# GpSimd pauses between bursts of gathers with a fill of its own, where it waited for the last gather to land

## The chip, the cores and the metric

The kernel runs on one core of a Trainium2 chip. A time is the device time of one execution in microseconds (us), and the program is compared by medians of several executions. One execution of the kernel was also recorded by the hardware profiler. Engines go by the names of the profile: PE is TensorE (PEld its weight loads), DVE is VectorE, ACT is ScalarE, POOL is GpSimd, SP is SyncE.

## The reference

A recommendation tower over a batch of 2048. Every sample has 40 ids, one for each of 40 embedding tables of 1,000 to 125,000 rows by 32 columns. All 780 pairs of fields are joined by a bilinear form, and the 780 results and 16 dense inputs go through a small network:

```
x  = stack([tbl_f[ids[:, f]] for f in range(40)])          # 2048 x 40 x 32
out = einsum('bpd,pde,bpe->bp', x[:, i], bilinear, x[:, j])  # 780 pairs i < j
y  = relu(relu([out, dense_ctx] @ W_top1 + b1) @ W_top2 + b2) @ W_top3
```

## The kernel before

The batch is cut into five **blocks** of 256, 512, 512, 512 and 256 rows (`ROWS`), numbered 0 to 4. The 40 fields are ten **chunks** of four fields, so that four times 32 columns fill 128 partitions. A **unit** is a pair of chunks, 50 in all; PE multiplies one chunk's transposed embeddings with the bilinear matrices (line 841, and 850 for a chunk with itself, into `U`), DVE multiplies the result with the other chunk's embeddings (line 740, `prod`), and PE sums that over partitions (line 866, `bank_z`). One such step over 512 columns is a **cycle**: 25 cycles in block 0, 50 in blocks 1 to 3, 25 in block 4, 200 in all. `summed` counts finished cycles. The network's layers (line 892) for a block are laid between the cycles of the next.

Embeddings come in two ways. Fourteen small tables lie in SBUF and are read by a product with a one-hot matrix, which DVE makes (line 704, `ones`) from the ids spread over the partitions (`idx_wide`, loads on SP's queue of up to 500 KB) and PE multiplies (line 792, `misc`). In block 0 seven of the fields come so, later all fourteen. All other fields are **gathered**: POOL issues an indirect DMA of 128 rows by 32 columns (line 505) for each field and each 128 samples, into the tile `rows`, which has seven slots (`R_SLOTS`). A slot holds one **turn**: the gathered fields of one chunk of one block. When all of a turn has landed (`gathered`), PE transposes it (line 815), and ACT copies the transpose to `x_T` (line 550), which the cycles read. There are 45 turns and 430 gathers. Turns 0 to 7 have eight gathers each and turn 8 has two (block 0). Blocks 1 to 3 have nine turns each of 16, 8, 8, 8, 16, 16, 12, 16 and 4 gathers, and block 4 half of that. So turn 1 is complete with gather 16, turn 2 with 24, turn 3 with 32, turn 4 with 40, turn 13 with 122, turn 14 with 138, turn 16 with 166 and turn 23 with 242.

What sets the order: each engine runs its instructions in program order. PE's order is written out (`TURN_AT` gives the cycle after which a turn is transposed), and a turn that has not landed stops everything that stands behind it on PE. POOL's order is that of the turns. It waits for three things: that PE has emptied a slot (`turned`), that PE has come to a cycle from which a field may be fetched (`summed`, the table `DUE`, from block 0's last turns on, some 0.8 of a block ahead of its use), and, behind every fourth gather but in turn 0 (`BURST = 4`), that this gather has landed. The first such wait stands behind gather 12; there are 105 of them.

SP issues all plain loads in one order: four small tables and the bilinear matrices `W`, most of them in rows of 128 bytes, then `idx_wide`, more tables, more of `W`, and from 69 us on the first layer's weights.

Of the kernel before, what the change touches and what calls it, by code (L numbers as in the profile page):

```python
# [12 lines left out]
P = 128  # L13
# [11 lines left out]
NB = max(ROWS)  # L25
# [243 lines left out]
X_SLOTS, R_SLOTS, P_SLOTS, Z_SLOTS, ONES = 12, 7, 6, 10, 4  # L269
# [12 lines left out]
def dlrm_tower(nc, dense_ctx, ids, tables, W_top1, b_top1, W_top2, b_top2, W_top3, bil, out):  # L282
    with ExitStack() as ctx:
        def sb(name, shape, dt=F32):
            return ctx.enter_context(nc.sbuf_tensor(name, shape, dt))

        def ps(name, shape):
            return ctx.enter_context(nc.psum_tensor(name, shape, F32))

        def sem(name):  # L290
            return ctx.enter_context(nc.semaphore(name))
# [22 lines left out]
        h1 = sb("h1", [P, H1 // P, NB])  # L314
        h2 = sb("h2", [P, H2 // P, NB])
        y = sb("y", [1, NB])

        prods = prod[:].rearrange("p s r n -> p (s r n)")
        spare_z = z[:, ZT:, :].rearrange("p s n -> p (s n)")
# [14 lines left out]
        bank_z = ps("bank_z", [P, NB])  # L334
        misc = ps("misc", [P, NB])

        ids_loaded, ids_rest_loaded = sem("ids_loaded"), sem("ids_rest_loaded")
        W_zeroed, stage_zeroed, W1_zeroed = sem("W_zeroed"), sem("stage_zeroed"), sem("W1_zeroed")
        late_stage_zeroed = sem("late_stage_zeroed")
# [11 lines left out]
        gathered = [sem(f"gathered{s}") for s in range(R_SLOTS)]  # L351
# [131 lines left out]
        @block.gpsimd  # L483
        def _(pool):
            nc.gpsimd.memset(ident[:], 0.0).then_inc(ident_made, 1)
            nc.gpsimd.iota(row_of_i[:], pattern=[[1, KC]], base=0, channel_multiplier=KC).then_inc(row_of_made, 1)
            pool.wait_ge(ident_made, 1)
            nc.gpsimd.affine_select(out=ident[:], in_=ident[:], compare_op=ALU.not_equal, fill=1.0, base=0,
                                    pattern=[[-1, P]], channel_multiplier=1).then_inc(ident_made, 1)
            pool.wait_ge(ids_loaded, 16)  # L490
            begun = [0] * R_SLOTS
            for n, (o, c) in enumerate(TURNS):
                if n == 1:
                    pool.wait_ge(misc_kept, JOB[("look", 0, 0)] + 1)
                if n >= R_SLOTS:
                    pool.wait_ge(turned, n - R_SLOTS + 1)
                for f in GATHERED[(o, c)]:
                    field = CF * CHUNK_OF_STEP[c] + f
                    if DUE[(o, c, f)]:
                        pool.wait_ge(summed, DUE[(o, c, f)])  # L500
                    if n == FIRST_TURN[1] and f == GATHERED[(o, c)][0]:
                        pool.wait_ge(ids_rest_loaded, 16)
                        pool.wait_ge(rows_zeroed, 1)
                    for t in range(ROWS[o] // P):
                        nc.gpsimd.indirect_dma_start(  # L505
                            out=rows[:, n % R_SLOTS, t, f, :], out_offset=None, in_=tables[field][:, :],
                            in_offset=bass.IndirectOffsetOnAxis(
                                ap=idx[:, OFF[o] // P + t, field:field + 1], axis=0),
                        ).then_inc(gathered[n % R_SLOTS], 16)
                        begun[n % R_SLOTS] += 1  # L510
                        if sum(begun) % BURST == 0 and n > 0:
                            pool.wait_ge(gathered[n % R_SLOTS], 16 * begun[n % R_SLOTS])

        @block.scalar
        def _(act):
# [26 lines left out]
            def keep_turn(o, c):  # L542
                n, N = TURN[(o, c)], ROWS[o]
                at = 2 * (U_USE[("turn", o, c)] % U_SLOTS)
                J = CHUNK_OF_STEP[c]
                if free_of(o, J):
                    act.wait_ge(multiplied, free_of(o, J))
                act.wait_ge(turned, n + 1)
                for _, lo, hi in pieces([CF * J + f for f in GATHERED[(o, c)]]):
                    last = nc.scalar.activation(x_of(o, J)[lo * DIM:hi * DIM, :], U[lo * DIM:hi * DIM, at, 0:N],  # L550
                                                ACT.Copy)
                last.then_inc(turn_kept, 1)
# [415 lines left out]
```

## Time and profile before

| | us |
|---|---|
| median of 3 runs | 867.06 (866.54 to 875.61) |
| profiled execution, its own time | 871.17 |
| its span, first to last instruction | 869.4 |
| PE matmuls busy | 779.0 |
| DVE busy | 586.5 |
| POOL busy (the gathers' issue) | 416.9 |
| ACT busy | 199.1 |
| mean granted TensorE clock | 0.941 |

The span is one execution; the 1.8 us between it and the execution's own time lie outside the first and last instruction. A gather's bar on POOL is the time in which its transfer is made up and issued; its data land later. The granted clock is 1.0 or 0.5 at any moment (2.4 or 1.2 GHz), and a figure between is a mean.

### The profile page before, as it was taken

Reading aid. Unit: us, or ns where it says so; the run is one execution under the profiler, and the core shown is the slowest. Engines: PE = TensorE matmul, PEld = TensorE weight load, DVE = VectorE, ACT = ScalarE, POOL = GpSimd, SP = SyncE. Lnnn points to the kernel's source line nnn. Section 1 sums busy time; section 2 is a strip of 40 time slices with the busy share of each in tenths; the row PEclk is TensorE's granted clock in tenths of the full one; section 3 lists DMA queues with packets and bytes.
Section 4 is the critical chain, followed back from the end, with each engine's and each line's share of the span. In section 5 each row is a group of like instructions: output and inputs, shape, how many; then the busy total and the mean of one; then the engine's idle time right before and its main releaser. Section 6 shows DMA issues by size and latency. Waiting matters only on the chain.

```text
span 869.4 us, 16025 instructions
## 1 busy us (share of the span) xinstructions
PE 779.0 (90%) x6766; PEld 308.5 (35%) x6766; DVE 586.5 (67%) x702; ACT 199.1 (23%) x362; POOL 416.9 (48%) x437
## 2 busy tenths in 40 slices
PE   3357888999679899989999999999999999999999
PEld 3124444443223233323323323323323234445446
DVE  5245766668448879857758679757768589566660
ACT  6022212232112023043021032132210221322212
POOL 5445456555656555555655565656565652310000
PEclk9567899799789999999999999999999999999999
DMA  4582330020010101020100101020100100000000
GB/s 90 115 114 52 68 69 11 11 29 17 14 25 11 33 12 27 12 35 11 28 11 12 34 11 28 12 24 12 19 12 12 23 11 16 8 5 2 2 1 1
DMA packets 62562, 22.53 MB, mean 26 GB/s; under 512 B 45283, under 2 KB 61677, under 8 KB 62490
## 3 DMA queue, kind: packets, MB, share of 16 engines
q1 hardware_dynamic: 48702, 14.37, 7.7%
q0 software_dynamic: 13760, 7.07, 6.9%
q8 instruction: 53, 0.87, 0.4%
q14 instruction: 19, 0.16, 0.1%
q10 hardware_dynamic: 28, 0.06, 0.0%
HBM read 21.40 MB, written 0.07 MB: 25 GB/s over the span
## 4 chain that ended last, share of the span: by engine, by line
PE 58%; POOL 15%; issue 11%; DMA 10%; DVE 3%; another core or an unknown queue 2%; ACT 1%; POOLq 0%; DVEq 0%; ACTq 0%
PE U L841 17%; PE bank_z L866 16%; POOL rows L505 15%; PE misc L892 14%; DMA rows<-in_tbl,idx 10%; PE misc L792 6%; DVE prod L740 2%; PE U L850 2%; PE U L892 2%; PE U L815 1%; DVE ones L704 1%; ACT x_T L559 0%; PE bank_z L874 0%; DMA idx<-in_ids 0%
## 5 line engine op out<-in xcount | busy, mean ns | idle before, releaser
L505 POOL DMA_INDIRECT rows<-in_tbl,idx x430 | 416.1, 968 | 351.0 <-DMA rows<-in_tbl,idx 203.0
L740 DVE TENSOR_TENSOR prod<-U,x_T 128x1024 f32<-128x1024 f32 (+1 forms) x314 | 342.6, 1127 | 102.4 <-PE U L841 84.5
L866 PE MATMUL bank_z<-prod,select 128*32 128x512 f32 (+1 forms) x2000 | 226.5, 540 | 4.0 <-ACT z L539 2.3
L841 PE MATMUL U<-x_T,W 32*128 32x512 f32 (+1 forms) x1440 | 203.6, 568 | 16.1 <-ACT x_T L550 9.3
L704 DVE TENSOR_SCALAR ones<-idx_wide,row_of 125x2048 bf16<-125x2048 f16 (+3 forms) x180 | 108.2, 627 | 63.4 <-PE misc L792 43.3
L792 PE MATMUL misc<-ones,tabs 125*32 125x512 bf16 (+1 forms) x1890 | 125.2, 356 | 7.0 <-issue 5.8
L740 DVE TENSOR_TENSOR prod<-U,x_look 128x1024 f32<-128x1024 f32 (+1 forms) x90 | 88.0, 1003 | 44.1 <-PE U L841 39.2
L841 PEld LDWEIGHTS U<-x_T,W 32*128 32x128 f32 x1440 | 79.0, 193 | 102.1 <-issue 52.1
L892 PE MATMUL misc<-z,W 128*128 128x512 f32 (+1 forms) x238 | 106.3, 561 | 0.6 <-ACT x_look L559 0.6
L866 PEld LDWEIGHTS bank_z<-prod,select 128*32 128x32 f32 x2000 | 46.8, 112 | 154.1 <-issue 110.8
L792 PEld LDWEIGHTS misc<-ones,tabs 125*32 125x32 bf16 x1890 | 65.2, 100 | 85.8 <-issue 55.8
L550 ACT ACTIVATE x_T<-U 32x512 f32<-32x512 f32 (+5 forms) x52 | 26.7, 514 | 235.5 <-PE U L815 149.9
L815 PE MATMUL U<-ident,rows 128*128 128x128 f32 x144 | 27.3, 306 | 44.9 <-DMA rows<-in_tbl,idx 43.2
L892 PEld LDWEIGHTS misc<-z,W 128*128 128x128 f32 x238 | 39.4, 189 | 66.8 <-issue 61.3
L539 ACT ACTIVATE z<-bank_z 128x512 f32<-128x512 f32 (+1 forms) x35 | 17.9, 512 | 180.2 <-PE bank_z L866 137.7
L841 PE MATMUL U<-x_look,W 32*128 32x512 f32 (+1 forms) x360 | 55.0, 551 | 0.3 <-DVE prod L740 0.3
L577 ACT ACTIVATE x_twin<-x_T 32x512 f32<-32x512 f32 (+1 forms) x80 | 43.4, 542 | 2.5 <-DVE prod L728 1.4
L815 PEld LDWEIGHTS U<-ident,rows 128*128 128x128 f32 x144 | 17.8, 153 | 67.1 <-issue 59.3
L892 PE MATMUL misc<-h,W 128*128 128x512 f32 (+3 forms) x80 | 37.6, 586 | 0.0
L722 DVE TENSOR_TENSOR prod<-U,x_T 128x512 f32<-128x512 f32 (+1 forms) x20 | 11.6, 579 | 38.3 <-PE U L850 28.7
L850 PE MATMUL U<-x_twin,W 32*64 32x512 f32 (+1 forms) x200 | 36.4, 607 | 0.1
L850 PE MATMUL U<-x_T,W 32*64 32x512 f32 (+1 forms) x160 | 28.9, 609 | 1.4 <-ACT x_twin L587 1.4
(70 smaller groups left out, 270.6 us busy)
## 6 DMA issues: line engine op xcount, KB each, us to landing
rows<-in_tbl,idx POOLq DMA_INDIRECT x430
idx_wide<-idx_rows SPq DMA_DIRECT2D x6, 500.0 KB
idx_wide<-idx_rows SPq DMA_DIRECT2D x6, 375.0 KB
idx_wide<-idx_rows SPq DMA_DIRECT2D x3, 187.5 KB
W<-in_W_top SPq DMA_DIRECT2D x35, 2.0 KB
W<-_L_rec_bilinear_matrices SPq DMA_DIRECT2D x4, 128.0 KB
W<-in_W_top SPq DMA_DIRECT2D x1, 512.0 KB
idx_wide<-idx_rows SPq DMA_DIRECT2D x2, 250.0 KB
```

The lines of the kernel that those rows point to most:

```text
L505: nc.gpsimd.indirect_dma_start(out=rows[:, n % R_SLOTS, t, f, :], out_offset=None, in_=tables[field][:, :], in_offset=bass.IndirectOffsetO ...
L539: nc.scalar.activation(z[:, at % Z_SLOTS, 0:ROWS[o]], bank_z[:, 0:ROWS[o]], ACT.Copy).then_inc(z_kept, 1)
L550: last = nc.scalar.activation(x_of(o, J)[lo * DIM:hi * DIM, :], U[lo * DIM:hi * DIM, at, 0:N], ACT.Copy)
L577: nc.scalar.activation(x_twin[r * DIM:(r + 1) * DIM, 1, 0:N], x_of(o, a + 1)[(CF - 1 - r) * DIM:(CF - r) * DIM, :], ACT.Copy)
L704: nc.vector.tensor_scalar(ones[:, n % ONES, 0:len(fs), 0:N], idx_wide[job % 2][:, 0:len(fs), 0:N], row_of[0:KP, k:k + 1], None, ALU.is_equ ...
L740: last = nc.vector.tensor_tensor(to[:, :, m * N:(m + n) * N].rearrange("p r (m n) -> p r m n", m=n), U[:, at:at + 2, m * N:(m + n) * N].re ...
L792: last = nc.tensor.matmul(misc[f * DIM:(f + 1) * DIM, 0:N], tabs[0:KP, LOOKED.index(field), part, k * DIM:(k + 1) * DIM], ones[:, n % ONES ...
L815: last = nc.tensor.transpose(U[:, at, t * P:(t + 1) * P], rows[:, n % R_SLOTS, t].rearrange("p f d -> p (f d)"), ident[:])
L841: last = nc.tensor.matmul(U[:, at + r % 2, m * N:(m + 1) * N], W[row, at_W:at_W + P], x_of(o, a)[row, :], start=True, stop=True, skip_grou ...
L850: last = nc.tensor.matmul(U[side * P // 2:(side + 1) * P // 2, at + r % 2, m * N:(m + 1) * N], W[row, at_W + side * P // 2:at_W + (side + ...
L866: last = nc.tensor.matmul(bank_z[r * DIM:(r + 1) * DIM, 0:N], sel, prod[:, (2 * g + r // 2) % P_SLOTS, r % 2, m * N:(m + 1) * N], start=(k ...
L892: last = nc.tensor.matmul(res, lhs, rhs, start=(t == 0), stop=(t == depth - 1), skip_group_check=True)
```

## The change

The wait for landing goes. In its place POOL fills a new tile `pause` of 128 x 512 float32 with zeros and waits until this fill is done, which a semaphore of its own (`paused`) tells. Nobody reads `pause`. The place is the same: behind every fourth gather but in turn 0, 105 times. The waits on `turned`, `summed` and the ids stay, and PE still waits for all gathers of a turn.

```diff
+        pause = sb("pause", [P, NB])
...
+        paused = sem("paused")
...
-            begun = [0] * R_SLOTS
+            begun, pauses = [0] * R_SLOTS, 0
...
                         if sum(begun) % BURST == 0 and n > 0:
-                            pool.wait_ge(gathered[n % R_SLOTS], 16 * begun[n % R_SLOTS])
+                            pauses += 1
+                            nc.gpsimd.memset(pause[:], 0.0).then_inc(paused, 1)
+                            pool.wait_ge(paused, pauses)
```

## Rows read from the trace of the kernel before

**Rows 1.** the page: the span, and who carries the chain that ended last

```profile
span 869.4 us, 16025 instructions
...
PE 58%; POOL 15%; issue 11%; DMA 10%; DVE 3%; another core or an unknown queue 2%; ACT 1%; POOLq 0%; DVEq 0%; ACTq 0%
```

**Rows 2.** PE's waits over the span: us in total, times, longest

```profile
PE U L815 <- DMA rows<-in_tbl,idx: 43.2, 7, 12.8
```

**Rows 3.** PE's timeline: turns' transposes: start us, us, what [idle before <-releaser]

```profile
38.10 0.66 PE L815 MATMUL U<-ident,rows 128*128 128x128 f32 x2 [12.82 <-DMA rows<-in_tbl,idx]
...
54.32 0.66 PE L815 MATMUL U<-ident,rows 128*128 128x128 f32 x2 [10.07 <-DMA rows<-in_tbl,idx]
...
68.59 0.41 PE L815 MATMUL U<-ident,rows 128*128 128x128 f32 x2
...
84.11 0.66 PE L815 MATMUL U<-ident,rows 128*128 128x128 f32 x2 [0.44 <-DMA rows<-in_tbl,idx]
...
226.99 0.87 PE L815 MATMUL U<-ident,rows 128*128 128x128 f32 x3 [8.49 <-DMA rows<-in_tbl,idx]
...
253.97 0.87 PE L815 MATMUL U<-ident,rows 128*128 128x128 f32 x3 [6.11 <-DMA rows<-in_tbl,idx]
...
305.02 0.63 PE L815 MATMUL U<-ident,rows 128*128 128x128 f32 x4 [3.24 <-DMA rows<-in_tbl,idx]
...
435.63 0.87 PE L815 MATMUL U<-ident,rows 128*128 128x128 f32 x3 [2.04 <-DMA rows<-in_tbl,idx]
```

**Rows 4.** GpSimd's timeline while the loads run: gathers 12, 13, 22 and 24

```profile
22.57 0.94 POOL L505 DMA_INDIRECT rows<-in_tbl,idx  x1 [0.30 <-issue]
28.65 0.94 POOL L505 DMA_INDIRECT rows<-in_tbl,idx  x1 [5.13 <-DMA rows<-in_tbl,idx]
...
47.13 1.40 POOL L505 DMA_INDIRECT rows<-in_tbl,idx  x1 [0.31 <-issue]
...
50.16 0.94 POOL L505 DMA_INDIRECT rows<-in_tbl,idx  x1 [0.30 <-issue]
```

**Rows 5.** GpSimd's timeline in a quiet stretch: one burst ends, the next starts

```profile
220.58 0.94 POOL L505 DMA_INDIRECT rows<-in_tbl,idx  x1 [0.30 <-issue]
223.21 0.94 POOL L505 DMA_INDIRECT rows<-in_tbl,idx  x1 [1.68 <-DMA rows<-in_tbl,idx]
224.46 0.95 POOL L505 DMA_INDIRECT rows<-in_tbl,idx  x1 [0.31 <-issue]
```

**Rows 6.** GpSimd's waits over the span, columns as in Rows 2

```profile
POOL rows L505 <- DMA rows<-in_tbl,idx: 203.0, 93, 5.3
...
POOL rows L505 <- PE bank_z L866: 37.8, 17, 5.0
```

**Rows 7.** GpSimd's timeline, first and eighth gather of turn 0

```profile
3.06 1.10 POOL L505 DMA_INDIRECT rows<-in_tbl,idx  x1 [1.65 <-DMA idx<-in_ids]
...
12.71 1.49 POOL L505 DMA_INDIRECT rows<-in_tbl,idx  x1 [0.30 <-issue]
```

**Rows 8.** GpSimd's timeline, two of its fills at the start

```profile
0.25 0.10 POOL L957 MEMSET const-float32-0.0<- 128x1 f32 x1 [0.25 <-issue]
...
0.74 0.20 POOL L485 MEMSET ident<- 128x128 f32 x1 [0.29 <-POOLq L957]
```

**Rows 9.** stretches: length, busy us by engine, granted clock, DMA share, GB/s

```profile
60.00:166.00 106.00, 88.05 (x956) 44.35 (x948) 69.80 (x103) 20.31 (x45) 57.01 (x59) 0.84 0.26 49
227.00:230.80 3.80, 3.80 (x16) 1.39 (x20) 0.60 (x1) 0.60 (x1) 1.84 (x2) 0.50 0.05 9
254.00:258.10 4.10, 4.10 (x28) 1.18 (x28) 1.00 (x2) 0.60 (x1) 1.16 (x2) 0.50 0.06 12
305.00:309.30 4.30, 4.28 (x29) 0.96 (x29) 1.85 (x3) 0.60 (x1) 1.73 (x2) 0.60 0.07 11
435.50:439.00 3.50, 3.37 (x24) 1.25 (x28) 0.23 (x1) 0.60 (x1) 0.94 (x1) 0.51 0.08 14
```

**Rows 10.** the page, costliest groups: VectorE's one-hot compares

```profile
L704 DVE TENSOR_SCALAR ones<-idx_wide,row_of 125x2048 bf16<-125x2048 f16 (+3 forms) x180 | 108.2, 627 | 63.4 <-PE misc L792 43.3
```

## The prediction, made before the result was known

> **What bounds the kernel now.** I read the page first. The chain that ended last is PE for 58% of the span, but POOL and the gathers' transfers hold 25% of it between them [rows 1]. A chain led by two sides asks for the places where they meet, so next come PE's waits: 43.2 us go to gathers that had not landed, in seven waits [rows 2]. PE's timeline shows where. Turn 1 costs 12.82 us, turn 2 10.07, turn 4 0.44, and later turns 13, 14, 16 and 23 cost 8.49, 6.11, 3.24 and 2.04 [rows 3]. Turn 3 costs nothing. From 436 us on no turn is waited for. So up to turn 16 POOL sets the pace at two places, the beginning and the middle of block 1, and PE sets it elsewhere and from there to the end.
>
> Why is POOL late? A gather occupies it for 0.94 us and the next begins 0.30 later; behind every fourth stands the gap in which it waits for landing. In a quiet stretch that gap is 1.68 us [rows 5]; while SP's loads run it is 5.13 [rows 4]. Over the span the waits that a landing ended make 203.0 us, 93 of them, 2.18 each, while waits for PE's progress make only 37.8 [rows 6]. A burst thus takes 4 x 0.94 + 3 x 0.30 + g = 4.66 + g, with g the gap. The change touches g alone.
>
> **The new gap.** It has three pieces: from gather to fill, the fill, from fill to gather. No row has a fill of 128 x 512. One of 128 x 1 took 0.10 us and one of 128 x 128 took 0.20 [rows 8]; the straight line through them gives 0.10 + 0.10 x 511/127 = 0.50, four times the larger 0.82. For the two joints I take at most the 0.30 that stands between gathers. So g lies between 0.50 (no joints) and 1.42 (0.82 + 0.60), and I take 0.50 + 0.60 = 1.1, because the line through both fills uses all that the trace has. The gain per burst is 0.6 us when quiet and up to 4 while loads run. The Trainium skill, page "SBUF — State Buffer", section "SBUF: two separate sides", gives GpSimd 4 bytes per lane and cycle at 1.2 GHz, so an estimate from that page is 512 / 1.2 GHz = 0.43 us for the fill; the sum would move by under half a microsecond.
>
> **First part, turns 1 to 4.** Gather 12 ends at 22.57 + 0.94 = 23.5 [rows 4]. Gather 16 then ends at 23.5 + 1.1 + 4.66 = 29.3 and gather 24 two bursts of 5.76 later, at 40.8. When do they land? Behind gather 12 it took 5.1 us from the end of its bar, behind gather 24 3.2 (bar's end 51.1, turn 2 at 54.32) [rows 3, 4]; in the quiet stretch 1.7 [rows 5]. I take 4.0, the middle of the two busy ones, and keep 1.7 and 5.1 as ends. Turn 2 then starts at 44.8 in place of 54.3. From turn 2 to turn 3 PE needed 68.59 - 54.32 = 14.3 us and waited for no gather; from 3 to 4 it needed 84.11 - 0.44 - 68.59 = 15.1 [rows 3]. That is PE's own work with its looks and cycles, and it becomes the bound here: turn 3 at 59.1 (gather 32 would have landed by 40.8 + 11.5 + 4 = 56.3), turn 4 at 74.2 (gather 40 by 67.8). **Gain 9.9 us.** Its ends: g 0.5 and landing 1.7 give 13.5, g 1.4 and 5.1 give 7.5. Of turn 1's wait of 12.82 and turn 2's of 10.07 more than half stays, since gathers at 1.25 us apiece are slower than the few cycles that PE has to do by then.
>
> **Second part, the later turns.** Gather 122, the last of turn 13, now ends 24.5 bursts behind gather 24, at 40.8 + 24.5 x 5.76 = 181.9. PE comes to turn 13 at 227.0 - 8.5 - 9.9 = 208.6, so it waits no longer, with 27 us to spare. Gather 166 (turn 16) ends at 245, PE comes at about 274; gather 242 (turn 23) at 355, PE at about 401. So all four waits go: 8.49 + 6.11 + 3.24 + 2.04 = **19.9 us**. What becomes late next is POOL's own gate: with gathers ahead, it waits for `summed`, as it did for 37.8 us before [rows 6]. That costs nothing, since this gate opens a good half of a block before the turn. The gain saturates here: any g up to about 2.0 removes these waits, because the 27 us are spread over 27.5 bursts. That makes the sum insensitive to the fill's length.
>
> **Third part, the clock.** Behind each of these four waits PE worked at the lower of its two clocks for a while: 227.0 to 230.8 at 0.50, 254.0 to 258.1 at 0.50, 305.0 to 309.3 at 0.60, 435.5 to 439.0 at 0.51 [rows 9]. It was busy all that time. Time at half clock is 3.8 + 4.1 + 4.3 x 0.8 + 3.4 = 14.7 us, and without the idle time ahead of it the same work takes half: **7.4 us**. Lower end 0. For turns 1 and 2 I take none back, since PE still idles ahead of them.
>
> **The sum.** 9.9 + 19.9 + 7.4 = 37.2 us. The profiled execution took 871.2, so a like one takes 834.0; it lay 4.1 above the median of 867.06, so the median becomes 829.9. I say 830. What lies outside the span is not touched. The fills themselves, 105 x 0.5 us, lie on POOL and in the place of a longer wait. `pause` has no reader and adds no work elsewhere.
>
> **Rivals.**
> *The start gives nothing.* Without the wait the gathers queue behind SP's loads, and landing, not issue, sets the pace of turns 1 and 2. For it: landing took up to 5.1 us there. Against it: turn 0's eight gathers went out with no wait, the eighth 9.65 us behind the first, 1.38 apiece against 1.24 [rows 7]. Only 19.9 + 7.4 remain: 840. Chance 0.12.
>
> *The clock gives more.* From 60 to 166 us the granted clock is 0.84 on average with PE busy 88.05 of 106 us [rows 9]; that is 34 us at half clock. If PE, less often halted, kept the full clock, up to half of that, 17 us, comes on top: 813. Against it: no gather is waited for between 85 and 218 us, so PE's idle bits there have other causes and stay. Chance 0.08.
>
> *Fills and one-hots hold each other up.* A gather at 47.13 took 1.40 us where 0.94 is usual [rows 4]; one-hot compares run close by. They are busy 108.2 of 869.4 us, 12% [rows 10]. The same page of the Trainium skill, section "Who interferes with whom", has VectorE's compares and copies in a two-port mode and GpSimd shut each other out for a whole instruction. As a mechanism of this kernel: 12% of 105 fills is 13 meetings, each worth at most a compare of some 0.63 us on average, 8 us in all if every one lay on the path: 838. DVE idles a third of the span, so most would be hidden. The 0.46 us by which that gather is longer agree with such a rule, and do not prove it. Chance 0.06.
>
> *The gap hardly shrinks.* If going from gather to fill and back costs POOL more than joints of 0.30, g can be near 2.4, the old mean, and nothing comes: 858 to 867. Chance 0.06.
>
> *Slower: the fill takes longer than the landing did.* Place: every burst up to turn 23. Before, turn 16 started at 305.0 [rows 3], so its gather 166 ended some 1.7 earlier, at 303.3; 38.5 bursts lie between gather 12 and it, so the old pace equals 4.66 + g with g = (303.3 - 23.5) / 38.5 - 4.66 = 2.6. This is the point from which it decides. At g = 3.0 turn 16 comes at 23.5 + 38.5 x 7.66 + 1.7 = 320, 15 later; the 19 bursts to turn 23 take 145.5 us against 130.6 before, 15 more; block 3, with slack before, adds about 10 (an estimate): 40 in all, 907. For it: no row shows a fill between gathers. Against it: the fill would have to take over 2 us, four times my line. Chance 0.08.
>
> **How the numbers follow.** My forecast, 822 to 838, has 0.60. The cases with the start's gain gone or the locks hold 0.18 and reach 840, with their own spread some 848; the clock's case reaches 813, less the spread 811. So 811 to 848 leaves out 0.06 + 0.08 and a little of the tails. About 1% is what a measurement of this kernel can tell from none: faster 0.85, within 1% 0.07, slower 0.08.
>
> **What the profile after would show.** Fills of about 0.5 us, and 1.1 us from the end of one burst to the next. Turn 1 near 33, turn 2 near 45, turn 4 near 74 us. No wait of PE for gathers after turn 2. On POOL, waits on `summed` (bank_z) that grow well beyond 37.8 us. A granted clock of 1.0 at what was 227, 254, 305 and 436 us. I am wrong if a fill with its joints takes over 2 us, if a gather's bar grows beyond 0.94 as more are in flight, or if PE, come earlier, meets something else that is late: `W` of a chunk or `idx_wide`, whose loads are not moved by the change.

## The result: slower on the measured chip, 890.86 us against 867.29

The changed kernel took 890.86 us (median of 4 runs, 887.7 to 895.35), the kernel before 867.29 us (4 runs, 866.54 to 875.61). The ratio is 1.0265, 95% interval 1.0193 to 1.0337: slower beyond the noise, though the interval does not settle whether by more than 2%. The forecast was 830 us, with a range of 811 to 848. The profiled execution took 891.69 us, its span is 889.9.

GpSimd did what the change asks of it. Its timeline in the changed kernel, the end of one burst and the start of the next:

```profile
33.52 0.94 POOL L507 DMA_INDIRECT rows<-in_tbl,idx  x1 [0.30 <-issue]
34.45 0.54 POOL L515 MEMSET pause<- 128x512 f32 x1
35.27 0.95 POOL L507 DMA_INDIRECT rows<-in_tbl,idx  x1 [0.27 <-issue]
...
39.96 0.54 POOL L515 MEMSET pause<- 128x512 f32 x1
```

The fill takes 0.54 us here (0.58 on average over all 105), it starts at once behind the gather, and 0.27 us lie between it and the next gather. The gap behind a burst is 0.81 us. A burst with its gap takes 39.96 - 34.45 = 5.51 us, or 1.38 us per gather. The old gap was 1.68 when quiet [rows 5].

PE's waits in the changed kernel (us in total, times, longest) and then GpSimd's:

```profile
PE U L845 <- ACT x_T L554: 20.5, 5, 13.9
PE U L845 <- issue: 14.3, 8, 5.8
PE U L819 <- DMA rows<-in_tbl,idx: 12.2, 2, 6.5
```
```profile
POOL rows L507 <- PE bank_z L870: 172.1, 70, 6.5
```

The waits for gathers fell from 43.2 to 12.2 us [rows 2], and only turns 1 and 2 are waited for. GpSimd now runs ahead until its own gate stops it, 172.1 us against 37.8 [rows 6]. Two new lines stand above: PE waits for ACT's copy of a transposed turn, and for "issue", which means that the profile shows no end of a wait. The chain that ended last says the same, and names a new holder:

```profile
PE 71%; another core or an unknown queue 14%; DVE 5%; ACT 4%; issue 4%; DMA 1%; DVEq 0%; ACTq 0%
```

POOL and the gathers' transfers held 25% of the old chain [rows 1] and are next to nothing in this one, whose 1% of DMA is put down to loads of `idx_wide`. "Another core or an unknown queue" held 2% and holds 14%, though the program runs on one core. The timelines show where that is. PE's, from turn 2 to the first cycles behind turn 3:

```profile
44.04 0.66 PE L819 MATMUL U<-ident,rows 128*128 128x128 f32 x2 [6.52 <-DMA rows<-in_tbl,idx]
50.50 2.11 PE L845 MATMUL U<-x_T,W 32*128 32x256 f32 x16 [5.80 <-issue]
...
73.07 1.01 PE L796 MATMUL misc<-ones,tabs 125*32 125x512 bf16 x5 [0.40 <-issue]
74.50 1.01 PE L796 MATMUL misc<-ones,tabs 125*32 125x512 bf16 x5 [0.42 <-issue]
75.93 0.64 PE L796 MATMUL misc<-ones,tabs 125*32 125x512 bf16 x4 [0.43 <-issue]
...
82.23 0.69 PE L819 MATMUL U<-ident,rows 128*128 128x128 f32 x2
96.78 2.11 PE L845 MATMUL U<-x_T,W 32*128 32x256 f32 x16 [13.86 <-ACT x_T L554]
```

ACT's, its copies of turns 2 and 3:

```profile
50.07 0.39 ACT L554 ACTIVATE x_T<-U 128x256 f32<-128x256 f32 x1 [16.96 <-remote]
...
96.34 0.38 ACT L554 ACTIVATE x_T<-U 128x256 f32<-128x256 f32 x1 [41.78 <-remote]
```

And GpSimd's over the same stretch, around its last gather ahead of the gate:

```profile
93.58 0.96 POOL L507 DMA_INDIRECT rows<-in_tbl,idx  x1 [0.30 <-issue]
101.01 0.94 POOL L507 DMA_INDIRECT rows<-in_tbl,idx  x1 [6.47 <-PE bank_z L870]
```

PE's transposes of turn 2 end at 44.70, and ACT, which has nothing else to do, copies them at 50.07. Those of turn 3 end at 82.92 and are copied at 96.34, that is 13.4 us later. GpSimd has issued gathers in bursts without a longer break since turn 0; its last one ends at 94.54, and ACT goes on 1.8 us behind it. The releaser is shown as "remote": the profile sees the semaphore change without an instruction that ends just then. In between PE also works thinly: four or five matmuls come every 1.43 us and then it stands, marked "issue". That mark must be read with care: the 5.80 us of it ahead of 50.50 ended 0.04 us behind ACT's copy (50.07 + 0.39), which this matmul needs, so it was a wait for ACT whose end the trace does not hold. VectorE waits for PE in the same way, `ones` "remote" 47.1 us in 12 waits, the longest 15.0. I call this the **hold** below.

So turn 3 came at 82.23 instead of the forecast 59.1, and PE was granted only half its clock from 60 to 100 us (0.50 in the windows 60 to 80 and 80 to 100, in which it was busy for 12.8 and 5.1 us of 20).

### The profile page after: what moved, and what is told of

Read it like the earlier page. It is cut to its first block, busy times and chain, and to the rows that moved or that the text cites. A ratio compares the mean times of both kernels' runs of the same rounds, so it can differ in the third digit from the quotient of the medians.

```text
span 889.9 us, 16130 instructions
## 1 busy us (share of the span) xinstructions
PE 791.1 (89%) x6766; PEld 311.7 (35%) x6766; DVE 592.2 (67%) x702; ACT 199.2 (22%) x362; POOL 481.1 (54%) x542
## 4 chain that ended last, share of the span: by engine, by line
PE 71%; another core or an unknown queue 14%; DVE 5%; ACT 4%; issue 4%; DMA 1%; DVEq 0%; ACTq 0%
PE U L845 22%; PE bank_z L870 20%; PE misc L896 15%; PE misc L796 8%; PE U L854 3%; DVE prod L744 3%; PE U L819 2%; PE U L896 1%; DVE ones L708 1%; ACT x_twin L581 1%; DMA idx_wide<-idx_rows 1%; ACT x_T L563 1%; ACT x_twin L584 0%; ACT x_T L554 0%
## 5 line engine op out<-in xcount | busy, mean ns | idle before, releaser
L507 POOL DMA_INDIRECT rows<-in_tbl,idx x430 | 419.9, 976 | 307.3 <-PE bank_z L870 172.1
L708 DVE TENSOR_SCALAR ones<-idx_wide,row_of 125x2048 bf16<-125x2048 f16 (+3 forms) x180 | 113.4, 657 | 83.6 <-remote 47.1
L796 PE MATMUL misc<-ones,tabs 125*32 125x512 bf16 (+1 forms) x1890 | 132.6, 364 | 7.1 <-issue 5.0
L896 PE MATMUL misc<-z,W 128*128 128x512 f32 (+1 forms) x238 | 108.5, 571 | 6.5 <-ACT x_look L563 6.3
L896 PEld LDWEIGHTS misc<-z,W 128*128 128x128 f32 x238 | 40.4, 193 | 74.2 <-issue 63.6
L515 POOL MEMSET pause<- 128x512 f32 x105 | 60.7, 578 | 0.1
L845 PE MATMUL U<-x_look,W 32*128 32x512 f32 (+1 forms) x360 | 58.0, 554 | 1.0 <-DVE prod L744 0.9
L543 ACT ACTIVATE z<-bank_z 128x512 f32<-128x512 f32 (+1 forms) x35 | 17.9, 512 | 175.4 <-PE bank_z L870 132.1
L819 PE MATMUL U<-ident,rows 128*128 128x128 f32 x144 | 26.1, 297 | 14.0 <-DMA rows<-in_tbl,idx 12.2
L854 PE MATMUL U<-x_T,W 32*64 32x512 f32 (+1 forms) x160 | 30.8, 573 | 1.6 <-issue 1.6
L845 PEld LDWEIGHTS U<-x_look,W 32*128 32x128 f32 x360 | 22.7, 188 | 24.5 <-issue 13.4
```

What stands on the lines that cost most here:

```text
L507: nc.gpsimd.indirect_dma_start(out=rows[:, n % R_SLOTS, t, f, :], out_offset=None, in_=tables[field][:, :], in_offset=bass.IndirectOffsetO ...
L515: nc.gpsimd.memset(pause[:], 0.0).then_inc(paused, 1)
L708: nc.vector.tensor_scalar(ones[:, n % ONES, 0:len(fs), 0:N], idx_wide[job % 2][:, 0:len(fs), 0:N], row_of[0:KP, k:k + 1], None, ALU.is_equ ...
L796: last = nc.tensor.matmul(misc[f * DIM:(f + 1) * DIM, 0:N], tabs[0:KP, LOOKED.index(field), part, k * DIM:(k + 1) * DIM], ones[:, n % ONES ...
L819: last = nc.tensor.transpose(U[:, at, t * P:(t + 1) * P], rows[:, n % R_SLOTS, t].rearrange("p f d -> p (f d)"), ident[:])
L845: last = nc.tensor.matmul(U[:, at + r % 2, m * N:(m + 1) * N], W[row, at_W:at_W + P], x_of(o, a)[row, :], start=True, stop=True, skip_grou ...
```

## The experiments

The same kernels behave differently from chip to chip, so each result names its chip by number (0, 4, 5, 7 or 12). Each ratio is to the kernel before, run in turns with it on the same chip. The chip of the first measurement is not on record. Chip 5 served two jobs and behaved alike in both; the others served one job each, so for them chip and moment are not told apart.

### First job, chip 5: the pace of the gathers

My theory was that PE's results are held up while gathers follow each other too closely.

**no_pause**: neither the wait nor a fill.

```diff
-                        if sum(begun) % BURST == 0 and n > 0:
-                            pool.wait_ge(gathered[n % R_SLOTS], 16 * begun[n % R_SLOTS])
```

> Neither the wait for landing nor the fill; gathers follow each other at 1.25 us apiece (the changed kernel: 1.37 on average, 5.5 for four with the fill). Pace theory: PE is held up whenever gathers follow each other closely for more than a few in a row, and in the changed kernel PE's bundles of matmuls came every 1.43 us in that state; at 1.25 us apiece it is held longer, so slower than the changed kernel's 891, I expect 895 to 920. Fill theory (the fill itself does the harm, by a lock or by its place on POOL): without fills the loss goes, 825 to 845.

Measured 782.06 us, ratio 0.913 (0.9096 to 0.9165). That lies outside both ranges. The fastest pace of all gave the best time: my theory, as it stood, fell.

**fill_each_256**: half the fill, behind every gather, 0.36 us each.

```diff
-                        if sum(begun) % BURST == 0 and n > 0:
+                        if n > 0:
                             pauses += 1
-                            nc.gpsimd.memset(pause[:], 0.0).then_inc(paused, 1)
+                            nc.gpsimd.memset(pause[:, 0:NB // 2], 0.0).then_inc(paused, 1)
```

> A fill of 128x256 behind every gather from turn 1 on, in place of one of 128x512 behind every fourth: 0.94 + 0.32 + 0.27, about 1.53 us from gather to gather, evenly spread, no wait for landing. Pace theory: 1.53 is above the 1.43 us at which PE's bundles came, so PE is hardly held up, and POOL is still faster than before (1.7 on average): 825 to 845. Landing theory (what matters is that a gather has landed, and the queue is empty, before more are issued while SP's loads run): as slow as the changed kernel, 880 to 900. Fill theory: four times as many fills, slower than 891.

Measured 822.41 us, 0.9604 (0.9564 to 0.9644), a little below the range of the theory of pace.

**four_fills**: four whole fills behind each burst.

```diff
+                            for _ in range(4):
-                            pauses += 1
-                            nc.gpsimd.memset(pause[:], 0.0).then_inc(paused, 1)
-                            pool.wait_ge(paused, pauses)
+                                pauses += 1
+                                nc.gpsimd.memset(pause[:], 0.0).then_inc(paused, 1)
+                                pool.wait_ge(paused, pauses)
```

> Four fills of 128x512 behind every fourth gather, 2.2 us in a row, about 7.1 us for four gathers (before: 6.4 when quiet, up to 9.8 while SP's loads run); no wait for landing. Pace theory: PE is held up as little as before; POOL's pace is near the old mean, so 855 to 875. Landing theory: slow at the start, 880 to 900. Fill theory: 420 fills in place of 105, over 900.

Measured 905.93 us, 1.0567 (1.0515 to 1.0619). PE waits 105.7 us for gathers in 17 waits. The range of the theory on the fill fits, but these waits are what grew: this is the plain price of slow gathers.

**wait_block0**: the landing wait in turns 1 to 8, fills from turn 9.

```diff
-                        if sum(begun) % BURST == 0 and n > 0:
+                        if sum(begun) % BURST == 0 and 0 < n < FIRST_TURN[1]:
+                            pool.wait_ge(gathered[n % R_SLOTS], 16 * begun[n % R_SLOTS])
+                        elif sum(begun) % BURST == 0 and n > 0:
                             pauses += 1
```

> The wait for landing stays for turns 1 to 8 (block 0, while SP's loads run), fills take its place from turn 9 on. Load theory (the harm is done by gathers in flight beside SP's loads): the start is as before, the later waits of PE for gathers go, 840 to 855. Pace theory: the start is as before, and from turn 9 on PE is held up as in the changed kernel, where it lost in block 1 what it gained at gathers: 860 to 880.

Measured 821.97 us, 0.959 (0.9544 to 0.9635), faster than both ranges. On this chip the kernels stand in the order of their gathers' pace, and the kernel before took 856 us, not 867. Either the recorded result was not of this kind of chip, or the changed kernel is odd. So it was run itself.

### Second job, chip 5: the changed kernel itself

> The changed kernel itself, once more. In the recorded run of it PE's semaphore updates came up to 14 us behind the end of its matmuls, and in the four experiments so far none came over 0.11 us late. Chip theory (those late updates belong to the chip or the moment on which the two kernels were first compared, and gathers without a pause for landing only make them worse): with no late updates here the working of the prediction holds, 812 to 830, ratio about 0.96. Kernel theory (one fill of 128x512 behind every fourth gather brings them about, which no experiment had from the start on): late updates again, ratio 1.02 to 1.03.

Measured 792.05 us, ratio **0.9244** (0.9222 to 0.9267). There are no late updates, as the chip theory has it, and it is 20 us below that theory's range.

> The kernel before, once more, for its trace beside after_again's. Chip theory: no update of PE over 0.2 us late (in the first trace up to 4 us, all through the span), and with that about 856, the median of before in the last job. Kernel theory: updates up to 4 us late as in the first trace.

Measured 857.0 us, 0.9997 (0.997 to 1.0023).

> No pause of either kind, once more, to see whether its 782 stands on this chip beside the changed kernel. Chip theory: if updates of PE are late here, it is hit harder than any other, since its gathers have no gap at all, and could be over 890; if they are not, 782 again. Pace theory on a chip without late updates: the faster the gathers, the better, no_pause 782, the changed kernel between it and before.

Measured 781.86 us, 0.9131 (0.9107 to 0.9155).

The same code that lost 2.7% gains 7.6% here. PE's timeline in the changed kernel on chip 5, from turn 2 to turn 3, and ACT's copies of these turns:

```profile
44.59 0.66 PE L819 MATMUL U<-ident,rows 128*128 128x128 f32 x2 [7.04 <-DMA rows<-in_tbl,idx]
45.72 2.11 PE L845 MATMUL U<-x_T,W 32*128 32x256 f32 x16 [0.47 <-ACT x_T L554]
...
54.93 2.13 PE L796 MATMUL misc<-ones,tabs 125*32 125x512 bf16 x36
56.98 0.44 PE L819 MATMUL U<-ident,rows 128*128 128x128 f32 x2
57.97 1.13 PE L845 MATMUL U<-x_T,W 32*128 32x256 f32 x8 [0.55 <-ACT x_T L554]
```
```profile
45.29 0.38 ACT L554 ACTIVATE x_T<-U 128x256 f32<-128x256 f32 x1 [11.75 <-PE U L819]
...
57.46 0.38 ACT L554 ACTIVATE x_T<-U 128x256 f32<-128x256 f32 x1 [7.68 <-PE U L819]
```

Turn 2 is transposed within 0.6 us of the other chip's, and copied when its transposes end. The releaser has a name, PE U L819. 36 matmuls of the looks come in one row of 2.13 us. Turn 3 stands at 56.98. No engine has a single wait that ends "remote" in any of the ten profiles taken on chips 5 and 7, and no copy of a turn by ACT starts over 0.10 us behind its transposes.

### Third job, chip 7: the two halves, and the fill's length

**fill_block0** is wait_block0 the other way round: fills in turns 1 to 8, the landing wait from turn 9.

> Fills for turns 1 to 8 (block 0), waits for landing from turn 9 on: the complement of wait_block0. Where no update of PE is late: wait_block0 kept the start of the kernel before and reached 822, the whole change 792; so the start is worth 30 and the rest 35, and this one should be 857 - 30 = 827, within 6, if the two parts add. If the waits of PE for gathers in block 1 only shift (a PE that is earlier meets the same late gathers), less: 840 to 850. If updates of PE are late again, both this and the changed kernel are above before.

Measured 826.38 us, 0.9644 (0.9597 to 0.9692). With wait_block0 the parts add up: 30.1 us from the start and 34.4 from the later turns (856.32 - 821.97, chip 5) make the 64 us of the whole.

**short_fill** has the whole change, with a fill of 128x1.

```diff
-                            nc.gpsimd.memset(pause[:], 0.0).then_inc(paused, 1)
+                            nc.gpsimd.memset(pause[:, 0:1], 0.0).then_inc(paused, 1)
```

> The changed kernel with a fill of 128x1 in place of 128x512: the gap behind a burst falls from about 0.81 us to about 0.4. The working of the prediction says that POOL's pace past turn 2 no longer matters, so only turns 1 and 2 come sooner, by 1 to 2 us: 790, and 782 (no pause) is the floor. Port theory (the fill's length holds VectorE up): most of the 10 us between the changed kernel and no pause comes back, 782 to 785.

Measured 781.82 us, 0.9132 (0.91 to 0.9164), the time of no_pause.

> The changed kernel once more, on whichever chip this job gets. If it is the same one as in the last two jobs: 792 again. If it is another: chip theory says that 792 (ratio 0.924) or 891 (ratio 1.03) comes with the absence or presence of late updates of PE in its trace, and with nothing in between.

Measured 792.99 us, 0.9256 (0.922 to 0.9292). So the length of the fill costs 11 us, about what I had put for a fill that holds VectorE up. Some of it is gathers that come later: PE waits 18.3 us for them against 12.5. Some is VectorE, whose largest compare is longer; with no fill at all (no_pause) it takes 770 ns. How the 11 us split between the two is not shown. Groups by shape, of short_fill and then of after_third:

```profile
L708 DVE TENSOR_SCALAR ones<-idx_wide,row_of 125x2048 bf16<-125x2048 f16 x60 | 44.2, 759 | 20.8 <-PE misc L796 15.1 <-DMA idx_wide<-idx_rows 5.7
```
```profile
L708 DVE TENSOR_SCALAR ones<-idx_wide,row_of 125x2048 bf16<-125x2048 f16 x60 | 46.9, 804 | 20.6 <-PE misc L796 15.1 <-DMA idx_wide<-idx_rows 5.4
```

### Fourth job, chip 4: the hold again

> The changed kernel once more, to meet the late updates of PE again. Two chips have given 792 and 793 with none over 0.2 us. Chip theory: if this job lands where updates are late, 885 to 895 and ratio 1.02 to 1.04; if not, 792 again.

Measured 898.77 us, **1.0294** (1.0236 to 1.0352). The kernel before took 874.56.

> No pause, beside it. Where updates of PE are late: if gathers that follow each other without a gap are what holds them, it is above the changed kernel, over 895; if it is the fills that hold them, it is below before. Where they are not late: 782 again, which tells nothing new.

Measured 902.79 us, 1.0348 (1.0286 to 1.041): the kernel that gained 8.7% on chips 5 and 7. Its PE timeline shows the hold at its purest; three of fifteen rows of one matmul each:

```profile
41.93 0.59 PE L790 MATMUL misc<-ones,tabs 125*32 125x512 bf16 x1 [2.54 <-issue]
44.73 0.59 PE L790 MATMUL misc<-ones,tabs 125*32 125x512 bf16 x1 [2.21 <-issue]
...
78.33 0.37 PE L813 MATMUL U<-ident,rows 128*128 128x128 f32 x1 [2.43 <-issue]
```

One matmul every 2.80 us, for 39 us. GpSimd's last gather ahead of its gate ends at 78.75. VectorE restarts at 86.78 and ACT at 87.07, both "remote", after 55.74 and 53.65 us without work. What grows is the gap ahead of the matmul. Its bar of 0.59 us, at a granted clock of 0.50, has an end that the profile models, so it can't show a slower matmul. The Trainium skill, page "SBUF — State Buffer", section "SBUF: two separate sides", says that a DMA cannot slow a compute instruction or the other way round. VectorE's bars agree: its products of 128x1024 from `x_T` took 1216 ns on average in the changed kernel both with the hold (first measurement) and without (chip 5). The page says nothing of the gap, which is what costs here.

### Fifth job, chip 12: what in the stream of gathers makes the hold

Open was whether the break's length, the pace, or SP's weight loads beside the first turns decides. The control told which kind of chip it was.

> The changed kernel, to tell which kind of chip this is. If TensorE's updates arrive late here: 1.027 to 1.030 of the kernel before, turn 3 transposed at 80 to 100 us. If they don't: 0.925, turn 3 at 57 us, and then the other three kernels of this job only repeat what they gave.

Measured 890.87 us, 1.0205 (1.0151 to 1.0259), a chip with the hold. The ratio is a little better than I had put it and turn 3 came at 70.70, ahead of the 80 to 100. Here the long wait stands behind it: ACT copied it at 95.1, 23.2 us behind its transposes.

> Four fills of 0.54 us behind each burst instead of one, so that GpSimd's break of some 2.9 us is longer than that of the landing wait, with no wait for a transfer in it. On a chip with late updates: if the length of the break is what lets TensorE's updates through, the first turns keep the time of the kernel before (turn 3 transposed at 65 to 75 us, no ScalarE copy over 4 us behind its transposes) and the ratio is the 1.057 of the other kind of chip or a little below, 1.04 to 1.06. If the landing wait itself is needed, turn 3 comes at over 80 us and the ratio is 1.06 to 1.10. On a chip without late updates: 1.057.

Measured 911.13 us, 1.0451 (1.0396 to 1.0506), turn 3 at 66.21. There is no landing wait in it, and the start keeps the old pace; the loss is PE's 87.9 us of waits for gathers. No copy by ACT came over 2.7 us late. Breaks made of fills do what the landing wait did.

> A fill of 128x256 (0.36 us) behind every gather: no bursts, breaks of some 0.6 us, the same average pace as with the landing wait. On a chip with late updates: if the break's length decides, none is long enough, turn 3 comes at over 75 us and the ratio is 1.00 to 1.05; if the pace decides, turn 3 comes at 60 to 65 us and the ratio is 0.96 to 0.98. On a chip without late updates: 0.960.

Measured 825.17 us, **0.9468** (0.9418 to 0.9518). "The break's length decides" fell: breaks of 0.6 us were enough, turn 3 stood at 64.66 us, and the ratio is a little better than the range that went with the pace. PE's waits for gathers are 34.5 us, and the chain is PE 73% with "another core or an unknown queue" at 0%.

> The landing wait in turns 1 to 8, fills from turn 9 on. On a chip with late updates: if the loss lies in the first eight turns (between turns 2 and 9 the changed kernel lost 47 us on the kernel before, and from turn 9 to the end it gained some 15 back), turn 9 comes where the kernel before has it, 176 us, and the ratio is 0.96 to 0.985. If the later stream loses as well, the ratio is 0.99 to 1.02. On a chip without late updates: 0.959.

Measured 908.34 us, 1.0415 (1.035 to 1.048). It lies beyond both ranges, and the theory that the loss lies in the first eight turns fell. The hold has no need of the start: it waited for the fills. GpSimd's timeline, its last landing wait and its first fill, and then PE's:

```profile
128.46 0.94 POOL L507 DMA_INDIRECT rows<-in_tbl,idx  x1 [1.65 <-DMA rows<-in_tbl,idx]
...
133.66 0.54 POOL L517 MEMSET pause<- 128x512 f32 x1
```
```profile
166.13 0.62 PE L798 MATMUL misc<-ones,tabs 125*32 125x512 bf16 x2 [0.78 <-issue]
167.54 0.59 PE L798 MATMUL misc<-ones,tabs 125*32 125x512 bf16 x1 [0.79 <-issue]
...
205.23 0.69 PE L856 MATMUL U<-x_look,W 32*64 32x256 f32 x2 [20.94 <-issue]
```

Up to turn 7 (135.8 us, before 138.7) it runs as the kernel before does. Turns 8 and 9 then come at 183.1 and 232.7, against 156.7 and 176.1. SP's weight loads beside the first turns are not what the hold needs.

### Sixth job, chip 0: average pace against the shape of the stream

Two kernels in which pace and shape are exchanged. **fill_each_128** is fill_each_256 with `pause[:, 0:NB // 4]`; **two_fills** is four_fills with `range(2)`. GpSimd's timeline of the first, and of the second:

```profile
34.01 0.95 POOL L507 DMA_INDIRECT rows<-in_tbl,idx  x1 [0.27 <-issue]
34.96 0.22 POOL L515 MEMSET pause<- 128x128 f32 x1
35.45 0.95 POOL L507 DMA_INDIRECT rows<-in_tbl,idx  x1 [0.27 <-issue]
```
```profile
30.80 1.03 POOL L507 DMA_INDIRECT rows<-in_tbl,idx  x1 [0.27 <-POOL pause L516]
...
35.59 1.12 POOL L516 MEMSET pause<- 128x512 f32 x2
36.98 1.28 POOL L507 DMA_INDIRECT rows<-in_tbl,idx  x1 [0.27 <-POOL pause L516]
```

That is 1.44 us per gather for the first, and (36.98 - 30.80) / 4 = 1.55 for this burst of the second, whose shortest bursts make 1.52.

> A fill of 128x128 (0.20 us) behind every gather: some 1.41 us per gather, evenly, against 1.39 us in the changed kernel's bursts. On a chip with late updates (the kernel before at 867 to 875 us): if the average pace decides, PE is held off as with the change, turn 3 at over 70 us, ratio 1.00 to 1.04; if a break behind every gather is what lets it through, turn 3 at 60 to 64 us, ratio 0.92 to 0.95. On the other kind (before at 856 to 857 us): 0.92 to 0.945.

Measured 880.83 us, 1.0134 (1.0093 to 1.0175), turn 4 at 96.55. Turn 3, at 65.51, came earlier than I had put it; from it to turn 4 PE took 31 us.

> Two 128x512 fills behind each burst of four: some 6.2 us per burst, 1.54 us per gather, the pace of the fill of 128x256 behind every gather (1.55) but in bursts with joints of 0.30 us. On a chip with late updates: if the average pace decides, turn 3 at 62 to 67 us and a ratio of 0.94 to 0.98; if the row of joints decides, turn 3 at over 72 us and a ratio of 1.00 to 1.04. On the other kind: 0.94 to 0.97.

Measured 838.32 us, 0.9621 (0.9553 to 0.9689), turn 3 at 58.17, which is before the range. Breaks behind every gather did not save the quick stream, and the rows of joints hardly harmed the slower one. **The average pace decides**, as far as these two can tell. Some hold is left in two_fills: "another core or an unknown queue" has 8% of its chain where fifth_fill_each has 0%, and ACT's latest copy came 5.4 us late against 1.8. They ran on different chips, and two_fills is also the quicker of the two at the start, so the shape may still have a small share.

The kernels by their pace, worked out from the starts of gathers four apart: the quickest four of the trace, and the median of those begun between 20 and 60 us, where SP's loads run. The ratios stand by the two kinds of chip:

| kernel | us per gather, quickest | median at 20 to 60 us | chips 5, 7 | chips with the hold |
|---|---|---|---|---|
| no pause | 1.25 | 1.25 to 1.30 | 0.913 | 1.035 (chip 4) |
| the change | 1.37 | 1.40 to 1.43 | 0.924, 0.926 | 1.021 to 1.029 (chip 12, first measurement, chip 4) |
| 128x128 behind each | 1.44 | 1.50 | not run | 1.013 (chip 0) |
| two fills per burst | 1.52 | 1.56 | not run | 0.962 (chip 0) |
| 128x256 behind each | 1.55 | 1.62 to 1.67 | 0.960 | **0.947** (chip 12) |
| landing wait (before) | 1.55 to 1.57 | 2.05 to 2.20 | 1 | 1 |
| four fills per burst | 1.81 | 1.89 to 1.92 | 1.057 | 1.045 (chip 12) |

The landing wait is slow only while loads run; in quiet stretches it has nearly the pace of the 128x256 fills. With the hold the best of the paces tried is 1.55, between two losses; without it faster is better until 1.25.

## Why the prediction was wrong, point by point

**The new gap, g = 1.1 us.** Measured 0.81. The fill was well placed, 0.54 for 0.50. The joints were taken at 0.30 each, and there is one of 0.27. Inside the ends of 0.50 and 1.42.

**Turns 1 and 2.** Forecast about 33.3 and 44.8; measured 30.91 and 44.04.

**Turn 3 at 59.1: the step that failed.** It says "That is PE's own work with its looks and cycles, and it becomes the bound here". PE took 82.23 - 44.04 = 38.2 us for it, not 14.3, and from turn 3 to 4 24.0 (106.2 - 82.2), not 15.1. From turn 4 to 13 it took 268.2 - 106.2 = 162.0, where 142.9 less the wait of 8.5 was expected, 134.4. These are 23.9 + 8.9 + 27.6 = 60.4 us, less the 0.8 by which turn 2 was early: 59.6, all ahead of turn 13. What stood against the assumption is the hold: on this kind of chip the time that PE needs is not its own, but depends on how closely gathers follow. On chip 5 the same stretch, turn 2 to turn 3, took 12.4 us.

**Turns 13, 14, 16, 23.** No wait for gathers in any of them, as forecast; the 19.9 us of waits are gone. The 27 us to spare were not all PE's to keep: without the hold PE comes to turn 13 at 181.2 instead of 208.6, and it waits 3.7 us for turn 14 on chip 5. From turn 13 to 23 the forecast is 208.6 less the waits of turns 14, 16 and 23 (11.4) and the clock's 5.7, that is 191.5. Measured on chip 5: 191.0. With the hold: 201.2, some 10 too long. From turn 23 to the end the changed kernel took 420.5 us, 11.6 less than the forecast's 433.8 - 1.7. On chip 5 the change needs 418.0 there and the kernel before 420.7. I read the 13 us more of the recorded kernel before as the hold at work in it too; no run tried that. 59.6 + 9.7 - 11.6 = 57.7, which is 889.9 less the forecast's span of 832.2.

**The clock.** Behind turns 13, 14 and 16 it was granted in full, 1.00 in the windows of 3.8 to 4.3 us there; behind turn 23 0.56. The 7.4 us came for the most part. The rival "the clock gives more" had it the wrong way round: from 60 to 100 us it fell to 0.50, where the hold left PE busy for 17.9 of 40 us.

**The rivals.** None of the five names the hold. "The start gives nothing" is refuted by fill_block0: the start alone gave 30 us on chip 7. "Fills and one-hots hold each other up" is small at most: with the longer fill the largest compares grew from 759 to 804 ns, which agrees with such a lock and does not prove it, and the whole length of the fill costs 11 us. "The gap hardly shrinks" and "the fill takes longer than the landing did" are refuted by the 0.54. The forecast's last sentence allows that PE "meets something else that is late". It named loads; it was PE's own results.

**Could it have been seen?** The kernel before has signs of it: its chain gives 2% to "another core or an unknown queue" in a program of one core [rows 1], and among VectorE's waits stands:

```profile
DVE ones L704 <- remote: 12.6, 9, 2.6
```

ACT has more: its waits for `x_T` that end "remote" make 54.4 us in 4, the longest 18.9. ACT's idle time costs nothing by itself, but its latest copy started 2.5 us behind the transposes, where chips 5 and 7 show at most 0.10. The prediction has no term for any of these. A wait that nobody's end explains should have had a term with an upper end, scaled with what the change speeds up.

**Without the hold the mechanism was right and the sum too small.** 64.5 us were gained on chip 5 and 63.5 on chip 7, for 37.2. The kernel before waits there 74.2 us for gathers in 12 waits, where the recorded one had 43.2 in 7: PE, not held, came earlier to turns 3, 7, 9, 10 and 11 and stood before gathers there too. In the changed kernel on chip 5 17.0 us of such waits are left, so 57 of the 64.5 us are such waits.

```profile
PE U L815 <- DMA rows<-in_tbl,idx: 74.2, 12, 13.5
```

**What stays open.** What in the chip is held: the runs show that other engines see PE's results late and that PE's instructions come in small groups, both at once, and that it ends behind a stream of gathers, 1.8 us behind the last one in the changed kernel and 8 us in the one with no pause. They don't show the path, nor why chips 5 and 7 are free of it. The gathers' data are not late with it: turn 2, which waits for its own, is transposed at 44.04 us with the hold and at 44.59 without. PE itself has no wait that ends "remote" in any profile, but some of its "issue" waits are waits for ACT without a record, as at 50.50.

The traces differ in one thing more. They hold 10,954 to 11,499 records of semaphore changes in the ten profiles of chips 5 and 7, and 5,432 to 8,078 in the ten of the chips with the hold, the program being the same. From 40 to 100 us the changed kernel has 347 in the first measurement and 1,896 on chip 5; in the first 20 us, before any hold, 299 and 515. Either changes are lost from the record or several are written as one; the runs don't tell. So "remote", "issue" and "another core or an unknown queue" may in part stand for missing records, and the late copies and starts are the firmer evidence. It also leaves a rival open: that the recording itself takes part in the hold. Every execution on record has a span and a granted clock, which come from recording, so none shows what these kernels take without it.

## What to carry to other kernels

A wait for landing behind a burst of indirect DMAs may guard more than its data: it sets the pace of the stream, and on some chips a quicker stream went with a starved TensorE. When such a wait goes, look on more than one chip for waits of other engines that are "remote" or "issue", and try a pace between, here 1.55 us per gather, which gained on both kinds (0.947 and 0.960), where no pause gives 0.913 or 1.035 according to the chip. A stretch in which an engine is shown to wait for nothing is not thereby work of its own. And before waits are compared across chips, count the records that the traces hold.

## What the hardware showed that was not expected

- While indirect DMAs of 128 rows follow each other at 1.25 us, PE on chip 4 gets one matmul every 2.80 us for 39 us. At 1.38 us, in the first measurement, ACT copied turn 3 13.4 us after its transposes had ended. At 1.55 us per gather the largest part is gone: the latest copy came 1.8 us late on chip 12 and 5.4 on chip 0.
- Chips of one type differ in this: chips 5 and 7 had none of it in ten profiles; chips 0, 4 and 12 and that of the first measurement had it, strongly or faintly, in all ten. The kernel before tells them apart only by 856 against 867 to 875 us.
- A fill of 128x512 float32 on GpSimd takes 0.54 us (0.58 on average), starts without a joint behind an indirect DMA, and the next DMA follows 0.27 us later.
